# The wide query product of the second layer in two triple parts per phase, at steps 2 and 5

## The reference

```
q_big  = einsum(x @ Wq.T, w_kc_q)            # 16 heads, 192 columns each
q_big  = rope(q_big);   kv_r = rope(ctx)
scores = (q_big @ W_qr) (kv_r @ W_kr).T      # 16 heads, 100 x 1444
ctx_c  = softmax(scores) @ kv_r
x      = x + (ctx_c @ w_kc_kv) @ Wo.T
x      = x + down(rms_norm(silu(gate(q8(x))) * up(q8(x))))   # weights of -1, 0, 1 and 8-bit inputs
```

## Time and profile before

| | |
|---|---|
| Median of three runs | 903.91 us (901.46 to 905.49) |
| Profiled execution | 904.72 us, span 903.0 us |
| TensorE matmul busy | 826.4 us (92%) |
| TensorE weight loads | 606.6 us (67%) |
| VectorE | 585.3 us (65%) |
| ScalarE | 397.2 us (44%) |
| GpSimd | 453.2 us (50%) |

### The profile page before, as it was taken

How to read it: one execution, slowest core, us unless ns; L and a number is a source line. 1 busy time by engine, 2 the same in 40 slices (tenths; PEclk the granted TensorE clock), 3 DMA queues, 4 the chain that set the end, 5 groups by cost and what they waited for, 6 DMA issues and landing times.

```text
span 903.0 us, 15604 instructions
## 1 busy us (share of the span) xinstructions
PE 826.4 (92%) x5844; PEld 606.6 (67%) x5844; DVE 585.3 (65%) x1133; ACT 397.2 (44%) x883; POOL 453.2 (50%) x465
## 2 busy tenths in 40 slices
PE   4998879999998799999999999999999999999883
PEld 3566656788887667677667677676767766765442
DVE  3437864213358675677878778778787787786545
ACT  2248852222231454544544454454354454444441
POOL 3000002800041187768776876776776776567630
PEclk9979996999999899999999999999999999999986
DMA  9532022789810100000000100000000000000000
GB/s 212 187 123 89 2 67 79 261 299 317 299 46 10 35 1 12 18 10 10 19 10 1 31 10 2 10 26 7 10 23 10 10 6 10 2 16 10 2 13 11
DMA packets 42168, 52.28 MB, mean 58 GB/s; under 512 B 12230, under 2 KB 35704, under 8 KB 41836
## 3 DMA queue, kind: packets, MB, share of 16 engines
q1 hardware_dynamic: 41068, 49.63, 17.5%
q0 software_dynamic: 1024, 1.64, 0.6%
HBM read 45.80 MB, written 5.36 MB: 57 GB/s over the span
## 4 chain that ended last, share of the span: by engine, by line
PE 68%; DVE 13%; ACT 7%; DMA 5%; issue 5%; SPq 1%; POOL 0%; POOLq 0%; ACTq 0%; DVEq 0%
PE ps L1197 14%; PE ps L1209 10%; PE ps L1177 7%; PE ps L1116 6%; PE ps L1121 3%; PE ps L1232 3%; DMA xs<-xs_scratch 3%; PE ps L1042 3%; PE ps L994 3%; PE ps L1143 3%; ACT sm L1465 2%; PE ps L1055 2%; DVE xyz L1947 2%; DVE xyz L1943 1%; PE ps L893 1%
## 5 line engine op out<-in xcount | busy, mean ns | idle before, releaser
L614 POOL TENSOR_TENSOR acc<-acc,pt 120x800 f32<-120x800 f32 (+1 forms) x157 | 299.1, 1905 | 94.4 <-ACT pt L1674 61.4
L1674 ACT ACTIVATE pt<-ps 120x400 f32<-120x400 f32 (+1 forms) x384 | 190.1, 505 | 222.5 <-PE ps L1197 211.6
L1976 DVE TENSOR_REDUCE nm<-ps 128x1 f32<-128x482 f32 (+1 forms) x336 | 213.7, 655 | 100.3 <-PE ps L1177 98.1
L1197 PE MATMUL ps<-qh,khl 128*120 128x400 f32 (+1 forms) x384 | 157.9, 411 | 11.1 <-ACT pt L1674 8.3
L1209 PE MATMUL ps<-pt,kv 120*64 120x400 f32 (+1 forms) x768 | 143.8, 510 | 0.0
L1177 PE MATMUL ps<-khl,qh 128*128 128x482 f32 (+1 forms) x336 | 131.6, 393 | 5.3 <-DVE nm L1976 4.6
L1197 PE MATMUL ps<-ql,kh 65*120 65x400 f32 (+1 forms) x384 | 134.3, 350 | 0.0
L1197 PEld LDWEIGHTS ps<-qh,khl 128*120 128x120 f32 (+1 forms) x384 | 70.9, 185 | 58.6 <-issue 32.4
L1209 PEld LDWEIGHTS ps<-pt,kv 120*64 120x64 f32 (+1 forms) x768 | 51.9, 138 | 65.8 <-issue 55.8
L636 POOL TENSOR_TENSOR rstd<-veps,mhalf 100x1 f32<-100x1 f32 (+2 forms) x20 | 13.4, 670 | 158.1 <-DVE veps L1808 114.6
L1197 PEld LDWEIGHTS ps<-ql,kh 65*120 65x120 f32 (+1 forms) x384 | 71.3, 186 | 5.1
(11 more groups left out here) (277 smaller groups left out, 1246.0 us busy)
## 6 DMA issues: line engine op xcount, KB each, us to landing
egu<-_L_ffn_gate_up_proj_dram SPq DMA_DIRECT2D x14, 1024.0 KB, 6.0
edn<-in_L_ffn_down_proj_dram SPq DMA_DIRECT2D x14, 512.0 KB, 7.1
spread<-inv_scratch SPq DMA_DIRECT2D x30, 100.0 KB, 2.7
craw<-in_ctx_dram SPq DMA_DIRECT2D x8, 360.0 KB
wo_n<-in_L_xattn_Wo_dram SPq DMA_DIRECT2D x1, 2048.0 KB, 10.5
wq_n<-in_L_xattn_Wq_dram SPq DMA_DIRECT2D x1, 2048.0 KB, 8.0
xs_scratch<-zero SPq DMA_DIRECT2D x1, 1792.0 KB, 9.9
xs<-xs_scratch SPq DMA_DIRECT2D x14, 128.0 KB, 6.1
```

The lines of the kernel that those rows point to most:

```text
L614: nc.gpsimd.tensor_tensor(total[r, :, :], before[r, :, :], pt[j % PT_BUF][r, :, :], ALU.add).then_inc(p_added, 1)
L1197: last = mm(ps[0:key_rows(t), k % 2, 0:HT], lhs[:, keys], rhs[:, HT * a:HT * a + HT], start=first, stop=not first)
L1674: nc.scalar.activation(pt[j % PT_BUF][0:rows, k % 2, :], ps[0:rows, k % 2, 0:HT], ACT.Exp).then_inc(p_ready, 1)
L1976: nc.vector.tensor_reduce(nm3[0:w, i, n:n + 1], ps[0:w, 3 + m % 2, 0:MN], AX.X, ALU.max).then_inc(m_reduced, 1)
```

## The change

Per phase the six parts are issued as three and three, at steps 2 and 5 of the phase, in place of two, two and two at steps 1, 3 and 5. The parts, their order and their number are the same.

```
-QB_AT = (1, 3, 5)
+QB_AT = (2, 5)
...
                     if u + 2 < NU and f < 2 and x in QB_AT:
-                        for part in range(2):
-                            q_big(u + 2, f, 2 * QB_AT.index(x) + part)
+                        for part in range(3):
+                            q_big(u + 2, f, 3 * QB_AT.index(x) + part)
```

## The result

The changed kernel takes 907.54 us at the median of 20 runs (899.63 to 912.45), the kernel before 905.05 beside it (20 runs). The ratio is 1.0047, 95% interval 1.0025 to 1.0070: slower by 2.3 to 6.3 us, where 1.0 us faster was forecast.

A forecast was written before the change was run, and what follows sets the result against it. TensorE's instruction order and its waits were taken to bound the kernel. The terms, 0 + 2.1 - 2.7 - 0.4, made it 1.0 us faster: 903.7 us from the profiled 904.72, 902.9 against the median of 903.91; range 900.0 to 906.0.

The forecast's parts named there:

- no waits on the maxima: Sign: TensorE's waits for VectorE's row maxima from 400 to 800 us should go from four to none.
- the wait on `ct`: Sign: TensorE's wait for VectorE at step 17, in phase 2 of even units, should stay at 0.8 us per batch.
- Term 1: Query product in phases 0 and 1: two runs of 12 in place of three of 8 cost nothing, 0 us.
- Term 2: Step 2 of phase 0, units 1 to 13: new wait on step 0's exponential, 13 times 0.16, 2.1 us slower.
- the other bare pairs come out just free: Steps 3 and 4, 8 and 9: 1.25 us against the 1.22 a score two steps on needs, so no wait.
- Term 3: Step 3 of phase 0 in odd units 5 to 13: the wait on VectorE's maxima goes, 2.7 us faster.
- Term 4: Small ones, 0.4 us faster: 0.2 from unit 0's rotation wait at step 9, 0.2 from TensorE jobs changing neighbours.
- A price per run: Rival, 14%: each query-product run has its own price, 0.09 saved 28 times, 2.5 us more, 900.4 us.
- No new wait: Rival, 8%: step 2 of phase 0 passes at once, 2.1 us more, 900.8 us.
- the wait of term 3 stays: Rival, 7%: VectorE's lateness in odd units moves along with TensorE; 2.7 us come back, 905.6 us.
- only the hidden loads count: Rival, 4%: fewer run entrances hide fewer weight loads, with no gain at exits; 3.1 us more, 906.0 us.
- VectorE binds at step 10: Rival, 10%: step 10's maximum product waits for step 8's reduction, late behind the rotation; 906.5 if 0.3 us late, up to 911.0.

The follow-up runs named there:

- Short exponentials: Against the changed kernel, exponentials of steps 0, 8 and 11 in units 2 to 13 take 32 of 400 columns; ratio to the kernel before 1.0017.
- the kernel with both instructions shortened: Changed kernel, units 2 to 13: exponentials and VectorE's reductions of steps 8 and 11 cut to 32 columns, step 0's exponential too; units 1 to 13 -1.60 us against kernel before.
- four and two: Kernel before, but phase 0 of odd units from 5 on issues four parts at step 1 and two at step 5; ratio 0.9972.
- the division early in all units: Four and two, plus VectorE's division of the context at step 14 in place of 15 in all units; ratio to the kernel before 0.9971.

## Why the prediction was wrong, step by step

Every sign that the prediction named came in: step 2 at 1.22, runs of 12 in 1.26, no waits on the maxima, the wait on `ct` unchanged, no matmul waiting at step 10. The forecast failed all the same, since none of them looks at the weight loads.

**Term 1 was right.** Runs of 12 and 16 cost what the line through 4, 8 and 24 says, 1.26 and 1.71 us.

**Term 2 is where it failed, twice.** It priced the new wait at step 2 "13 times 0.16": the delay of the waiting product's start, without the load that the wait lays bare behind it. The even units lose 0.26 on the average; in the odd ones 0.06 more come from a pair of bare steps (unit 1) or from the transposes of step 27, which now have a run's exit of their own. Over 13 units that is some 3.8 us in place of 2.1, if units 5 to 13 pay what unit 3 does. And "the other bare pairs come out just free" compared 1.22 with 1.25 from matmul start to matmul start. The load has to be ahead of its matmul as well, 0.11 more, which makes 1.33; at steps 10 and 13 the pairs fall short and lose 0.06 to 0.07 each, 1.66 us over 13 units that the sum had at nothing. Short exponentials alone did not bring this back, since the loop through the reduction is as long there; the kernel with both instructions shortened takes just this away. Unit 14 of the kernel before had the 0.11 in its trace, in the start of the second score product, 0.29 behind the first; the sum used it for the wait on the maxima (0.6 "with its tail") and not here.

```profile
812.21 0.45 PE L1197 MATMUL ps<-qh,khl 128*121 128x400 f32 x1
812.50 0.34 PE L1197 MATMUL ps<-ql,kh 65*121 65x400 f32 x1
```

**Term 3 was right in kind and a little small:** phase 0 of units 5, 7, 9 and 11 comes out 0.67 below that of units 1 and 3 (-0.35 against +0.32) and unit 13's 0.39 below, 3.1 us in all in place of 2.7.

**Term 4 was wrong in sign.** The neighbours gave nothing that shows, and unit 0 is 0.56 longer instead of 0.2 shorter. Its phase 0 is 0.86 longer, with triple parts there alone as well: step 6 stands for a maximum, 0.67 us, behind other work that VectorE has only there. What would free it was not tried. Its phase 1 is 0.30 shorter, but that is no gain of the change: in two kernels that leave unit 0 as it was (four and two, and that with the division early in all units) it came out 0.24 and 0.35 shorter, since the wait of 0.16 at step 9 is not in every execution.

The terms as measured: 0 + 3.8 + 1.7 - 3.1 = 2.4 for units 1 to 13 (2.46 by the starts) and 0.6 for unit 0, 3.0 us slower, inside the measured interval of 2.3 to 6.3. The 1.2 us up to its middle, 4.2, are not explained by the steps.

**The rivals.** A price per run fell: runs of 12 and 16 lie on the line. "No new wait" fell, and so did "the wait of term 3 stays" and "only the hidden loads count". "VectorE binds at step 10" had the place and half of the mechanism. The reduction does hold the load back there, by its own pace and not behind the rotation, beside the exponential, and at step 13 as well. Its point of decision, 0.04 us, was again reckoned without the load.

## What to carry to other kernels

Work that looks like filler between dependent steps can be what keeps a two-buffer loop off the critical path: before gathering it, compare the loop's whole length (product, consumer, release and the weight load behind the release) with two bare steps. Look for TensorE's waits in the weight loads too; small ones stand there alone. If the aim is to cover one late event, put more of the work ahead of it only where the event is late, as four parts at step 1 of the odd units did.

## What the runs showed that was not expected

At step 2 a wait on TensorE cost its delay and then a weight load: 0.29 us between the two score products behind it, where 0.18 is usual. And two loops of different engines stood level at steps 10 and 13: shortening ScalarE's alone left them at 1.91 us, shortening VectorE's as well brought 1.84. With the division early in all units, a stand of 1.89 us in unit 1 was followed by score products 0.33 apart at a granted clock of 0.50, the 1.2 GHz level.
